# Latent attention's keys and values rotated and split during the first MoE, kept in DRAM and loaded per batch; all probability additions on GpSimd

## What is computed

```python
def _L1_xattn_ref(hidden_q, kv_c, Wq, w_kc_q, w_kc_kv, W_qr, W_kr, Wo):
    q_hk = (hidden_q @ Wq.T).reshape(Bv, Sv, H, K)
    q_big = jnp.einsum('bshk,hkq->bshq', q_hk, w_kc_q)
    q_big = _apply_rope(q_big, sin_q[None, :, None, :], cos_q[None, :, None, :])
    sin_k, cos_k = _rope_tables(Lv, D_C)
    kv_r = _apply_rope(kv_c, sin_k[None], cos_k[None])
    q_r = jnp.einsum('bshq,hqr->bhsr', q_big, W_qr)
    k_r = jnp.einsum('bld,hdr->bhlr', kv_r, W_kr)
    scores = jnp.einsum('bhsr,bhlr->bhsl', q_r, k_r)
    attn = jax.nn.softmax(scores, axis=-1)
    ctx_c = jnp.einsum('bhsl,bld->bhsd', attn, kv_r)
```

## Time and profile before

| | |
|---|---|
| median of 3 runs | 1550.4 us (1540.61 to 1554.96) |
| span of the profiled execution | 1563.7 us, 21601 instructions |
| TensorE's mean granted clock | 0.964 of full |
| PE busy | 1450.8 us (93%) |
| weight loads (PEld) busy | 1100.7 us (70%) |
| DVE busy | 935.0 us (60%) |
| POOL busy | 789.6 us (50%) |
| ACT busy | 630.5 us (40%) |

### The profile page before, as it was taken

How to read it: one execution, slowest core, us unless ns; L and a number is a source line. 1 busy time by engine, 2 the same in 40 slices (tenths; PEclk the granted TensorE clock), 3 DMA queues, 4 the chain that set the end, 5 groups by cost and what they waited for, 6 DMA issues and landing times. The chain is left out here.

```text
span 1563.7 us, 21601 instructions
## 1 busy us (share of the span) xinstructions
PE 1450.8 (93%) x7635; PEld 1100.7 (70%) x7635; DVE 935.0 (60%) x1619; ACT 630.5 (40%) x1151; POOL 789.6 (50%) x621
## 2 busy tenths in 40 slices
PE   7788999899989999999999998988999998899998
PEld 4455566566646676676766755567988887899998
DVE  2752112466686768767686753577878774444554
ACT  2432221344423434424244342456666653333333
POOL 3732002367647769768677673057565551233332
PEclk9998999799999899989989999999999999999999
DMA  8014113510011101011010000101010001443441
GB/s 306 1 44 142 34 38 86 179 53 24 1 39 57 58 0 58 1 58 58 1 57 7 14 1 14 71 28 33 23 55 1 28 1 42 120 119 120 121 121 52
DMA packets 60321, 88.66 MB, mean 57 GB/s; under 512 B 7556, under 2 KB 44612, under 8 KB 60230
## 3 DMA queue, kind: packets, MB, share of 16 engines
q1 hardware_dynamic: 59206, 85.82, 17.2%
q0 software_dynamic: 1024, 1.64, 0.4%
HBM read 81.92 MB, written 5.41 MB: 56 GB/s over the span
## 5 line engine op out<-in xcount | busy, mean ns | idle before, releaser
L1007 ACT ACTIVATE prob<-PS 121x800 f32<-121x800 f32 x192 | 158.1, 837 | 254.0 <-PE PS L2041 238.3
L1405 DVE TENSOR_REDUCE mx<-PS 128x1 f32<-128x482 f32 (+1 forms) x312 | 186.7, 649 | 56.6 <-PE PS L2019 54.6
L622 POOL TENSOR_TENSOR e_wl<-e_wf,e_wh 128x768 fp32r<-128x768 f32 x33 | 71.0, 2151 | 174.4 <-ACT e_wh L905 152.6
L717 POOL TENSOR_TENSOR hT<-hT,prob 121x800 f32<-121x800 f32 x56 | 109.7, 1958 | 71.1 <-ACT prob L1007 68.9
L2018 PE MATMUL PS<-kth,qs 128*128 128x482 f32 (+1 forms) x312 | 131.5, 422 | 13.7 <-DVE mx L1405 10.3
L2056 PE MATMUL PS<-prob,kvn 121*64 121x400 f32 (+1 forms) x768 | 136.1, 503 | 0.9 <-ACT prob L1007 0.9
L717 POOL TENSOR_TENSOR xc<-xc,prob 121x800 f32<-121x800 f32 x56 | 114.8, 2050 | 30.3 <-ACT prob L1007 25.8
L2019 PE MATMUL PS<-kl,qm 66*128 66x482 f32 (+1 forms) x312 | 125.4, 402 | 0.0
L2038 PE MATMUL PS<-qs,kth 128*121 128x400 f32 (+1 forms) x384 | 113.1, 377 | 3.1 <-ACT prob L1007 2.4
L2041 PE MATMUL PS<-qm,kl 66*121 66x400 f32 (+1 forms) x384 | 105.4, 357 | 0.0
L2056 PEld LDWEIGHTS PS<-prob,kvn 121*64 121x64 f32 (+1 forms) x768 | 52.3, 137 | 71.2 <-issue 69.0
(11 more groups left out here) (301 smaller groups left out, 3650.1 us busy)
## 6 DMA issues: line engine op xcount, KB each, us to landing
e_wb<-routing SPq DMA_DIRECT2D x32, 400.0 KB, 3.9
wgu<-in_L_ffn_gate_up_proj SPq DMA_DIRECT2D x8, 1024.0 KB, 14.3
krt<-in_ctx_T SPq DMA_DIRECT2D x8, 722.0 KB, 4.1
ksw<-in_ctx_Tswap SPq DMA_DIRECT2D x8, 722.0 KB, 5.8
wdn<-in_L_ffn_down_proj SPq DMA_DIRECT2D x8, 512.0 KB, 7.9
wq<-in_L_ffn_Wq SPq DMA_DIRECT2D x4, 1024.0 KB, 5.3
wo<-in_L_ffn_Wo SPq DMA_DIRECT2D x4, 1024.0 KB, 5.7
e_wf<-in_L_ffn_Wg SPq DMA_DIRECT2D x32, 128.0 KB, 2.2
```

The lines of the kernel that those rows point to most:

```text
L622: pool.tensor_tensor(m["wl"][:, slot], m["wf"][:, slot], m["wh"][:, slot].bitcast(fp32), ALU.subtract).then_inc(ms["wlo"], 1)
L717: pool.tensor_tensor(acc, acc, prob[:, n % RING], ALU.add).then_inc(xb["ap"], 1)
L1007: act.activation(prob[0:k, n % RING], PS[0:k, 2 * (n % 2):2 * (n % 2) + 2, 0:GC], ACT.Exp).then_inc(xb["ex"], 1)
L1405: dve.tensor_reduce(mx3[:, m, g:g + 1], PS[:, 4 + k % 3, 0:SEG[g][1]], AX.X, ALU.max).then_inc(xb["free"], 1)
```

## The change

The rotated and split keys and the rotated values no longer come into being in the attention. They are made during the tile loop of the first MoE, stored in DRAM (`keys_d`, `values_d`), and loaded for each batch.

In the MoE stage two batches' keys lie one above the other on 128 partitions (a pair, four in all), in buffers that are otherwise idle there (`keyx`, `keys_`). VectorE multiplies, adds and subtracts in two halves of 722 columns, between the tile instructions; ScalarE rounds the sum into `keys_`; VectorE's remainder goes back into `keyx`. The values of a batch take three VectorE instructions of 121x768 and have two pairs of buffers. GpSimd's queue issues all of these loads and stores; the loads of a pair wait until both stores of the pair before have landed, those of a batch's values until the store of the batch two before. SP loads the tables after the routing. In the attention SP loads three pieces of 361 KB for each batch into three buffers of `kth` and `kl2`, and one for the values. VectorE's additions and `accd` are gone: GpSimd adds all 12 tiles (11 additions), and the column sums read `accp`. The three fills of ones now all stand at the head.

```diff
+        keyx, keys_ = (t_.rearrange("p c t -> p (c t)")[:, 0:SK] for t_ in (xc, sq))
+        valx = [t_[0:KP, 0:KT * DC] for t_ in (held0, held1)]
+        vals_ = [t_[0:KP, KT * DC:2 * KT * DC] for t_ in (held0, held1)]
...
+            def load_keys(b):
+                half_, ld = slice((b % 2) * DC, (b % 2 + 1) * DC), xb["ldk"][b % 3]
+                for lo in (0, DC):
+                    sp.dma_start(kth.bitcast(fp32)[lo:lo + DC, b % 3, :], keys_d[b // 2, 0, half_, :]).then_inc(ld, 16)
+                sp.dma_start(kl2[b % 3].bitcast(fp32)[0:DC, :], keys_d[b // 2, 1, half_, :]).then_inc(ld, 16)
 
             def load_values(b):
-                sp.dma_start(kvn[:, b % 2], a["ctx_N"][b]).then_inc(xb["ldn"], 16)
-                sp.dma_start(kvs, a["ctx_Nswap"][b]).then_inc(xb["ldn"], 16)
-            for tab, src in ((kcosT, "rope_kcosT"), (ksinT, "rope_ksinT"), (kcosN, "rope_kcosN"), (ksinN, "rope_ksinN")):
-                sp.dma_start(tab[:], a[src]).then_inc(xb["tab"], 16)
-            load_turned(0)
-            load_values(0)
+                sp.dma_start(kvn[:, b % 2].rearrange("p t d -> p (t d)"), values_d[b]).then_inc(xb["ldn"][b % 2], 16)
...
+            sp.wait_ge(rk["st"], 16 * 2 * NP)
+            sp.wait_ge(rk["vst"], 16 * B)
+            for b in range(2):
+                load_keys(b)
+                load_values(b)
...
-                if b + 2 < B:
-                    sp.wait_ge(xb["kl"], 3 * (b + 2))
-                    load_turned(b + 2)
-                if 0 <= b < B - 1:
-                    sp.wait_ge(xb["nrot"], 3 * (b + 1))
-                    if b > 0:
-                        sp.wait_ge(xb["pv"], 4 * b)
+                if b < 0:
+                    load_keys(2)
+                elif b + 2 < B and b > 0:
+                    sp.wait_ge(xb["s"], SP_ * b)
+                    load_keys(b + 2)
+                if 1 <= b < B - 1:
+                    sp.wait_ge(xb["pv"], 4 * b)
                     load_values(b + 1)
...
+            def load_turned(k):
+                if k:
+                    pool.wait_ge(rk["st"], 32 * k)
+                pool.dma_start(keyx, a["ctx_T"][k]).then_inc(rk["ld"], 16)
+                pool.dma_start(keys_, a["ctx_Tswap"][k]).then_inc(rk["ld"], 16)
+            def store_turned(k):
+                pool.wait_ge(rk["hi"], RHI + 2 * k + 2)
+                pool.dma_start(keys_d[k, 0], keys_).then_inc(rk["st"], 16)
+                pool.wait_ge(rk["lo"], RLO + 2 * k + 2)
+                pool.dma_start(keys_d[k, 1], keyx).then_inc(rk["st"], 16)
+            def load_natural(v):
+                ld = rk[f"vld{v % 2}"]
+                if v >= 2:
+                    pool.wait_ge(rk["vst"], 16 * (v - 1))
+                pool.dma_start(valx[v % 2], a["ctx_N"][v].rearrange("p t d -> p (t d)")).then_inc(ld, 16)
+                pool.dma_start(vals_[v % 2], a["ctx_Nswap"][v].rearrange("p t d -> p (t d)")).then_inc(ld, 16)
+            def store_natural(v):
+                pool.wait_ge(rk["vrot"], 3 * v + 3)
+                pool.dma_start(values_d[v], valx[v % 2]).then_inc(rk["vst"], 16)
+            load_turned(0)
+            pool.wait_ge(ms0["sc"], 16 * B)
+            load_natural(0)
+            load_natural(1)
+            for k, done_ in enumerate(((0,), (1, 2), (3,), (4, 5, 6, 7))):
+                store_turned(k)
+                if k + 1 < NP:
+                    load_turned(k + 1)
+                for v in done_:
+                    store_natural(v)
+                    if v + 2 < B:
+                        load_natural(v + 2)
+            pool.wait_ge(rk["st"], 32 * NP)
+            pool.wait_ge(rk["vst"], 16 * B)
...
-                if 7 <= u < 25 and u % 2:
-                    rotate_turned(0, (u - 7) // 2)
-                elif u in (25, 27, 29):
-                    rotate_values(0, (u - 25) // 2)
...
-            def add_probabilities(b, s):
-                n, t, i = b * SP_ + s, s % KT, b * 2 + s // KT
-                if t == 0 or ADDS[t] is None:
-                    return
+            def add_probabilities(i, t):
+                n, acc = i * KT + t, accp[i % 2]
                 pool.wait_ge(xb["ex"], n + 1)
-                acc = accp[i % 2]
                 if t == 1:
                     if i >= 2:
-                        pool.wait_ge(xb["ad"], 3 * i - 3)
+                        pool.wait_ge(xb["sums"], i - 1)
                     pool.tensor_tensor(acc, prob[:, (n - 1) % RING], prob[:, n % RING], ALU.add).then_inc(xb["ap"], 1)
                 else:
-                    pool.wait_ge(xb["ap"], 8 * i + ADDS[t] - 1)
-                    pool.tensor_tensor(acc, acc, prob[:, n % RING], ALU.add).then_inc(xb["ap"], 1)
-            for n in range(9):
-                rotate_turned(1, n)
-            for b in range(B):
-                turns = iter(range(9))
-                for s in range(SP_):
-                    add_probabilities(b, s)
-                    if b + 1 < B and s in (7, 8):
-                        for k in ((0, 1) if s == 7 else (2,)):
-                            rotate_values(b + 1, k)
-                    if b + 2 < B:
-                        for _ in range({12: 2, 15: 2, 17: 1, 19: 2, 21: 1, 23: 1}.get(s, 0)):
-                            rotate_turned(b + 2, next(turns))
+                    r = key_rows(t)
+                    pool.wait_ge(xb["ap"], (KT - 1) * i + t - 1)
+                    pool.tensor_tensor(acc[0:r], acc[0:r], prob[0:r, n % RING], ALU.add).then_inc(xb["ap"], 1)
+            for i in range(2 * B):
+                for t in range(1, KT):
+                    add_probabilities(i, t)
...
+            def high_turned(k, c):
+                act.wait_ge(rk["rot"], 6 * k + 3 * c + 3)
+                act.activation(keys_[:, CH[c]].bitcast(fp32r), keyx[:, CH[c]], ACT.Copy).then_inc(rk["hi"], 1)
             for i in range(NT):
                 tile_gate(i)
                 if i >= 1:
                     keep_hidden(i - 1)
                 if i + 1 < NT:
                     keep_tokens(i + 1)
+                if 1 <= i <= 3 * NP and i % 3:
+                    high_turned(i // 3, i % 3 - 1)
...
-                        high_keys(b + 1, 0)
                         high_queries(b + 1)
-                        high_keys(b + 1, 1)
-                        high_keys(b + 1, 2)
...
+            def rotate_turned(k, c):
+                if c == 0:
+                    dve.wait_ge(rk["ld"], 32 * (k + 1))
+                dve.tensor_tensor(keys_[:, CH[c]], keys_[:, CH[c]], ksinT[:, CH[c]], ALU.mult).then_inc(rk["rot"], 1)
+                dve.tensor_tensor(keyx[:, CH[c]], keyx[:, CH[c]], kcosT[:, CH[c]], ALU.mult).then_inc(rk["rot"], 1)
+                dve.wait_ge(rk["rot"], 6 * k + 3 * c + 2)
+                dve.tensor_tensor(keyx[:, CH[c]], keyx[:, CH[c]], keys_[:, CH[c]], ALU.add).then_inc(rk["rot"], 1)
+            def low_turned(k, c):
+                dve.wait_ge(rk["hi"], RHI + 2 * k + c + 1)
+                dve.tensor_tensor(keyx[:, CH[c]].bitcast(fp32r), keyx[:, CH[c]], keys_[:, CH[c]], ALU.subtract).then_inc(rk["lo"], 1)
+            def rotate_natural(j):
+                v, x, w = j // 3, valx[j // 3 % 2], vals_[j // 3 % 2]
+                if j % 3 == 0:
+                    dve.wait_ge(rk[f"vld{v % 2}"], 32 * (v // 2 + 1))
+                    dve.tensor_tensor(w, w, ksinN[:], ALU.mult).then_inc(rk["vrot"], 1)
+                elif j % 3 == 1:
+                    dve.tensor_tensor(x, x, kcosN, ALU.mult).then_inc(rk["vrot"], 1)
+                else:
+                    dve.wait_ge(rk["vrot"], j)
+                    dve.tensor_tensor(x, x, w, ALU.add).then_inc(rk["vrot"], 1)
             for i in range(NT):
                 tile_product(i)
                 if i >= 2:
                     keep_output(i - 2)
+                k = i // 3
+                if i == 0:
+                    dve.wait_ge(rk["tab"], RTAB + 64)
+                if k < NP and i % 3 < 2:
+                    rotate_turned(k, i % 3)
+                if k < NP and i % 3 >= 1:
+                    low_turned(k, i % 3 - 1)
+                if k < NP and i % 3 == 1:
+                    rotate_natural(4 * k)
+                if k < NP and i % 3 == 2:
+                    for j in range(1, 4):
+                        rotate_natural(4 * k + j)
+                if i >= 3 * NP:
+                    for j in range(4):
+                        rotate_natural(4 * (NP + i - 3 * NP) + j)
...
-            dve.memset(kl2[DC:DC + 2, 0].bitcast(fp32), 1.0).then_inc(xb["one"], 1)
-            for g in range(3):
-                low_keys(0, g)
+            for n in range(3):
+                dve.memset(kl2[n].bitcast(fp32)[DC:DC + 2, :], 1.0).then_inc(xb["one"], 1)
...
-                    if s == 2 and more:
-                        for g in range(3):
-                            low_keys(b + 1, g)
...
-                    if s in (0, 5) and b >= 1:
-                        add_probabilities(2 * b - 1, s)
```

(49 more changed lines are left out.)

87 lines of the change are left out of this document (17 added, 70 removed).

## The result

The changed kernel takes 1560.2 us in the median of 17 runs (1550.3 to 1567.2), the kernel before 1548.1 in 17 runs (1536.5 to 1555.1). The ratio is 1.0071, 95% interval 1.0049 to 1.0093: the change costs 11 us by the ratio, 0.7% (the two medians lie 12 us apart). That is inside the range of the prediction and inside its "within 1%", but the sum said zero, and the loss is clear of the interval. Both terms of the sum are there, with the signs that were forecast; the attention's gain is smaller than forecast and the MoE's loss larger.

A forecast was written before the change was run, and what follows sets the result against it. TensorE was taken to set the pace, losing time in the attention to waits and low clock. 25.7 us won there and 26 lost in the first MoE summed to 0 on the 1550.4 median: 1550 us, range 1528 to 1571.

The forecast's parts named there:

- Both terms of the sum: Attention 25.7 us won, first MoE 26 us lost, together 0 us.
- six times 4.15 us: Attention: six batch periods fall from 64.35 to 60.2 us, 25 us won, bounds 23 to 29.
- two stalls with two causes: Attention: TensorE waits 2.1 us for maxima behind VectorE's key subtractions, 1.8 us behind its probability addition; both causes go.
- the head: Attention's start: VectorE makes three fills of 1.26 us before TensorE's first product, 1.3 us lost.
- Rival 4: Attention: GpSimd's additions come late for the column sums, 30 us come back, 1580 us; chance 0.06.
- R: First MoE: round trip from a pair's last VectorE subtraction through store and load to the next keys, 12.6 us.
- The first tile's loads: First MoE: tile loads share the engines with the first keys, 1 us lost.
- the key chain: First MoE: subtraction, store, load, rotation, next product; a cycle of 22.7 us against 17.5 for three tiles.
- The end: End of MoE tiles: values of batches 6 and 7 wait for store and load; TensorE starts 4 to 5 us later.
- (1): First MoE: round trips hidden at 7.3 us or below, only some 6 us lost at its end, 1530 us; chance 0.21.
- (2): First MoE: round trip of 9.8 us, loss 18 us, sum -8, 1542 us; chance 0.2.
- Rival 3: First MoE: transfers queue, round trip 18.7 us, loss 43 + 1 us, sum +19, 1569 us; chance 0.15.

The follow-up runs named there:

- x_before: The kernel before, unchanged, profiled a second time and timed again: 1545.8 us, ratio 1.0011.
- x_adds: Changed kernel rotating only one key pair and two batches of values, probability additions divided as in the kernel before: 1547.6 us, ratio 1.0000.
- x_addsonly: Kernel before with only the probability additions all moved to GpSimd, rotations and key work left in the attention: 1576.4 us, ratio 1.0210.
- x_order: Changed kernel with first loads ahead of the token scatter and third pair's key stores ahead of a values reload: 1544.6 us, ratio 0.9981.

## Why the prediction was right and wrong

**The attention's gain: 25.7 forecast, 18 measured.** The step that failed is the largest term, "six times 4.15 us", and in it the start: "I put the sum on the median". I had seen that the profiled execution lay 0.9% above the median and took its period of 64.35 us for the typical one all the same. The second profile shows 61.95: of the 18.5 us between the two profiles 14.4 are in the stage, with its low-clock stretches, from which the term was taken. A gain worked out from an execution may not hold more of such loss than the median's kernel has. The other end of the period was mis-sized the opposite way: 59.0, where I took 60.2 and gave 59.55 as the least. That bound was TensorE's busy time in a batch, and it is no floor: in the period of before without a dip TensorE is busy 59.5 us,

```profile
857.73:918.28 60.55, 59.49 (x312) 41.64 (x313) 44.09 (x62) 21.85 (x30) 41.26 (x21) 1.00 0.05 13
```

and in the changed kernel 352.2 us in six periods, 58.7 each, for as many matmuls. 6 x (61.95 - 59.0) is 17.7, the measured gain. Of it 9.1 us are time in which TensorE stood still (10.9 us in the six periods of x_before, 1.8 after) and some 4 the lower clock. The rest, about 5 us, lies in TensorE's busy time, and no run shows its cause by itself. TensorE's weight loads waited longer for maxima before, in x_before and in the changed kernel (last figure):

```profile
L2018 PEld LDWEIGHTS PS<-kth,qs 128*128 128x128 f32 x312 | 61.5, 197 | 32.3 <-DVE mx L1405 21.9
```

```profile
L2022 PEld LDWEIGHTS PS<-kth,qs 128*128 128x128 f32 x312 | 61.1, 196 | 19.4 <-DVE mx L1438 7.0
```

**The mechanism there was half right.** The stalls of the earlier trace rows had their causes as told, and none is left: TensorE's waits for maxima come to 0.2 us, by the row of the first maxima product (busy and mean, then TensorE's idle time before it by cause):

```profile
L2022 PE MATMUL PS<-kth,qs 128*128 128x482 f32 (+1 forms) x312 | 125.9, 404 | 5.4 <-DVE kl L1478 3.2 <-ACT qm L1001 1.9 <-DVE mx L1438 0.2
```

The same row prices the head: 3.2 us of waiting for the three fills, 2.3 more than the 0.9 of before, where 1.3 more were forecast. The prediction named two stalls with two causes, as if either could be removed. x_adds and x_addsonly show that in these two kernels another stall takes the place of the removed one unless both parts are made.

**GpSimd's additions cost nothing, right.** TensorE has no wait for column sums in the changed kernel, and an addition takes 1.90 us in the mean. Rival 4 is out for this change. Where the rotations stay on GpSimd, x_addsonly shows it pacing the attention, though by rotations that come late and not, as in rival 4, by late column sums.

**The MoE's loss: 26 forecast, 29 measured.** VectorE's waits before pairs 1, 2 and 3 were all there, put down to a DMA. R was 12.3 and 11.2 us against the forecast 12.6, but 19.6 the third time. The terms were mis-sized in both directions. The first tile's loads cost 6.7 us, not 1: VectorE's product of tile 3 starts at 178.20 instead of 171.55. The third trip cost 7 us more, by the queue order that x_order mends (R there 13.3); the prediction named the key chain but did not walk GpSimd's queue for what stands ahead of it. The three trips together took 43.1 us where 37.8 were forecast. The end cost less: TensorE's shared product comes 27.9 us after the end of tile 10's product (241.09 to 268.97), where it was 27.3, so 0.6 us were lost where the prediction had 4 to 5, and 3 more for the low clock. That the sum of the term came so near is partly luck: about 11 us too little at the first tile and in the trips, some 7 too much at the end.

```profile
268.97 1.58 PE L1800 MATMUL PS<-sact,wsd 128*128 128x400 f32 x4 [1.11 <-DVE yt L1301]
```

**The rivals.** The round trips were not hidden (1) and R was not 9.8 (2). Rival 3's R of 18.7 came once in three times, and for its reason, transfers behind others, though by the order in one queue. The estimate of 9.1 us from the Trainium skill (DMA: Bandwidth & Descriptors, Anatomy of one DMA) is near for the store, 3.7 against 3.9 and 4.2 measured in the median, and short for the two loads, 5.4 against 7.0 from the first one's issue to the second one's landing in the first trip.

**The sum.** -18 and +29 make the 11 us, a small loss where none was forecast. A sum of two terms of 26 us and opposite sign says "no change" only as surely as the larger error in either; 8 us in the first and 3 in the second were enough. Neither bound by which it called itself wrong was crossed (an attention gain under 15 us, an MoE loss under 10 or over 40).

## What to carry to other kernels

Before a gain is taken from one profile, compare its span with the runs: if it lies above them, find the stage with the excess, and do not count what is peculiar to that execution. An engine's busy time in a profile is no floor for a period: here it fell with the waits around it. Work that fits beside a busy TensorE by its time is free only if nothing in its in-order queue waits: give each store-and-reload cycle more room than its round trip, and walk every queue in order for what stands ahead of a transfer. When two stalls lie close together, removing one may only bring on another; judge parts of a change together and apart.

## What was not expected of the hardware

A direct DMA keeps GpSimd busy for 0.53 to 0.62 us, half of the 1.1 that an indirect one takes. A VectorE addition with two inputs in SBUF that met a running GpSimd addition ended 0.85 us after that one, however early it had started (2.5 and 1.0 us long). Two executions of one program differed by 18.5 us, 14.4 of it in one stage, with a mean granted clock of 0.964 and 0.973. What decides which execution gets the longer stretches at 1.2 GHz no run here shows; the changed attention, without those stalls, kept its 59.0 us period in every profile.
